# A four-layer graph network on one core: the layout of each stage hands out dense steps for longer past the planned end of the edge work (OVERHANG 3000 to 15000)

## The reference, cut to what matters

```
h = relu(layernorm(x)); x = x + gcn(h)      # weighted sum over edges, degrees of src
h = relu(layernorm(x)); x = x + sage(h)     # two SAGE convolutions, mean over dst
h = relu(layernorm(x)); x = x + mlp(h)      # message MLP per edge, mean over dst, update MLP, layernorm
h = relu(layernorm(x)); x = x + mean(h)     # mean over src, two matrices
```

## Time and profile before

| | us |
|---|---|
| median of three runs | 5219.02 |
| lowest, highest run | 5215.02, 5253.27 |
| the profiled execution, span from first to last instruction | 5223.6 |

### The profile page before, as it was taken

The page is one execution under the profiler, slowest core; times in us unless marked ns, Lnnn a source line. Parts: engine busy times, 40 slices in busy tenths (PEclk is TensorE's granted clock), DMA queues, the critical chain, the costliest instruction groups (busy, mean ns, idle before and its releaser), DMA issues. The chain is left out here.

```text
span 5223.6 us, 87376 instructions
## 1 busy us (share of the span) xinstructions
PE 3895.7 (75%) x22802; PEld 3063.3 (59%) x22802; DVE 4158.1 (80%) x20654; ACT 3626.8 (69%) x9152; POOL 3880.5 (74%) x3228
## 2 busy tenths in 40 slices
PE   5517877778676668999868978989788886666654
PEld 4415666666455556877756766766566665554443
DVE  7628999999999997777758878888799997766564
ACT  0027989888666766777758877878678886766564
POOL 6777787885677766888866777776588775777777
PEclk9868999999777788999989989999899998878777
DMA  9966777776666665666658889988466663333332
GB/s 229 321 192 191 197 211 203 195 201 159 161 152 154 147 139 143 164 152 158 143 136 260 237 224 245 247 236 210 126 147 144 144 139 74 102 98 98 96 96 62
DMA packets 891584, 878.75 MB, mean 168 GB/s; under 512 B 131160, under 2 KB 671714, under 8 KB 891016
## 3 DMA queue, kind: packets, MB, share of 16 engines
q1 hardware_dynamic: 546568, 575.48, 34.2%
q0 software_dynamic: 224000, 235.91, 26.1%
q10 hardware_dynamic: 120514, 61.79, 4.6%
HBM read 345.71 MB, written 533.16 MB: 168 GB/s over the span
## 5 line engine op out<-in xcount | busy, mean ns | idle before, releaser
L1206 POOL DMA_INDIRECT node<-sage_comb,leadd x400 | 644.7, 1612 | 203.5 <-DMA node<-sage_comb,leadd 104.0
L460 PE MATMUL dense_p<-ident,dense_h 128*128 128x128 f32 x1956 | 336.0, 300 | 373.4 <-ACT dense_h L454 367.1
L454 ACT ACTIVATE dense_h<-dense_x,dense_n_shift,dense_n_rstd 128x128 f32<-128x128 f32 x1304 | 534.8, 487 | 89.1 <-DVE dense_n_shift L443 85.7
L460 PEld LDWEIGHTS dense_p<-ident,dense_h 128*128 128x128 f32 x1956 | 239.8, 151 | 475.7 <-ACT dense_h L454 454.0
L1206 POOL DMA_INDIRECT sums<-mlp_same,leadh x200 | 325.2, 1626 | 139.0 <-issue 80.2
L1206 POOL DMA_INDIRECT node<-gcn_comb,leads x200 | 326.3, 1632 | 105.3 <-issue 49.2
L1206 POOL DMA_INDIRECT sums<-mean_comb,leads x200 | 328.0, 1640 | 95.8 <-DMA sums<-mean_comb,leads 45.7
L470 PEld LDWEIGHTS dense_p<-wT,dense_hT 128*128 128x128 f32 x2608 | 378.8, 209 | 22.8 <-issue 7.4
L470 PE MATMUL dense_p<-wT,dense_hT 128*128 128x128 f32 x2608 | 377.1, 292 | 0.0
L451 ACT ACTIVATE dense_n_std<-dense_n_mean_var,eps 128x4 f32<-128x4 f32 x652 | 188.8, 294 | 216.1 <-DVE dense_n_mean_var L437 213.9
L1041 ACT ACTIVATE dense_hT<-dense_p 128x512 f32<-128x512 f32 x489 | 286.2, 589 | 63.8 <-PE dense_p L460 60.8
(11 more groups left out here) (310 smaller groups left out, 14374.1 us busy)
## 6 DMA issues: line engine op xcount, KB each, us to landing
node<-b SPq DMA_DIRECT2D x400, 256.0 KB
sums<-zero_row SPq DMA_DIRECT2D x400, 256.0 KB
node<-zero_row ACTq DMA_DIRECT2D x50, 1152.0 KB
dense_x<-in_x SPq DMA_DIRECT2D x163, 256.0 KB, 3.3
out<-dense_y SPq DMA_DIRECT2D x163, 256.0 KB
x_src<-xs SPq DMA_DIRECT2D x50, 256.0 KB, 5.7
y_dst<-gcn_y SPq DMA_DIRECT2D x50, 256.0 KB, 3.1
sage_xs<-x_src SPq DMA_DIRECT2D x50, 256.0 KB, 3.9
```

Source lines behind the costliest of these rows:

```text
L454: tiles(lambda t: nc.scalar.activation(out[:, t, :], x[:, t, :], func, bias=b.sh[:, t:t + 1], scale=b.rs[:, t:t + 1])).then_inc(done, 1)
L460: return tiles(lambda t: nc.tensor.transpose(ps[:, t * P:(t + 1) * P], x[:, t, :], ident))
L1206: pool.indirect_dma_start(table, bass.IndirectOffsetOnAxis(ap=leads[:, i * G + c, t:t + 1], axis=0), e.comb[c][:, t, :], None, element_off ...
```

## The change

```diff
 PATIENCE = 100
-OVERHANG = 3000
+OVERHANG = 15000
```

## The result

The changed kernel took 5322.82 us (median of five runs, 5316.02 to 5352.36) against 5219.02 before: a ratio of 1.0179 with a 95% interval of 1.014 to 1.0218 (the ratios of this document are taken over the sets of runs; the quotient of the two medians is 1.0199). It is slower by 104 us, which lies outside the range and on the side of my third rival. The profiled execution has a span of 5350.6 us and was the slowest of the five, so differences between the two traces add up to 127 us, not 104. TensorE's clock isn't what differs: averaged over an execution the granted clock was 0.879 to 0.884 after, and 0.881 to 0.886 in the thirteen executions of the kernel before that ran beside experiments 1 to 4. (In experiment 3 it was 0.873 to 0.875, in experiment 6 0.885 to 0.887, and both are slower than before.)

What follows compares the result with a forecast made beforehand. POOL, nearly full in every stage, was taken as the bound, DVE as second limit. 5223.6 + 35 (ends) - 19 (mean) + 0 (re-laid plans) = 5239.6 us, less 4.6 above the median: 5235, range 5195 to 5285.

Steps and rivals of the forecast that it cites:

- third rival: A re-laid sage2 falls badly, its chain of adds not catching up: 61 us more, 5296 us; chance 0.22.
- The ends: Longer dense tails delay barriers: gcn +13, sage1 +13, sage2 0, mlp +9; together +35 us, bounds +31 and +41.
- cover: At sage2's end, POOL's last three groups of adds hide the 13 us of added dense work, so cost 0.
- DVE's stop: At sage2's end, DVE's idle 26.82 us should be cut to about 14.
- the term that I set to 0, the re-laid plans: sage1 to mean laid out anew from shifted dense streams; each stage taken to last as before, 0 us.
- Mean's slack of 37 us: Mean's edges last 687.8 us against 650.9 of POOL's busy time and minimum idle time.
- sage2's 18 us: Slack of sage2's edges: 660 us against 642 of POOL's busy time and minimum idle time.
- The bounds that I drew: Re-laid stages as tight as sage2: sage1 -61, mlp -66; as loose as sage1: sage2 +61, mean +43, mlp +20.
- the sign that this term decides: First gather to last add moving by over 20 us in sage1, sage2 or mlp: the re-laid-plans term decides.
- the sign that the gain is wrong: Mean's POOL gap, 21.25 us, should fall to about 9.4; staying over 15 means the gain is wrong.
- Mean's end: Four dense rounds fewer let dense work end some 94 us before the edges; next gather 12 us earlier.
- the edges would go faster in mean (-7): With mean's last 94 us free of dense steps, two groups of adds wait less for ACT: -7 us.

Runs made afterwards that it cites:

- experiment 1: Kernel before with its orders kept, only the dense steps of 12 more planned us moved ahead of the barrier at four ends: 5244.98 us against 5221.72, ratio 1.0036.
- Experiment 2: Changed kernel with its orders kept, but the added dense tails run after the barrier, at the next stage's front: 5311.26 us against 5221.72, ratio 1.0149.
- experiment 3: Kernel before, overhang 3000, each due time shifted by a fixed pseudo-random -100 to +100 ns: 5364.76 us against 5221.72, ratio 1.025.
- experiment 4: Kernel before with an overhang of 4000 in place of 3000: 5326.74 us against 5221.72, ratio 1.0165.
- experiment 6: Changed kernel (overhang 15000) with new due times for sage1 to mean, fitted by a search: 5279.7 us against 5227.39 for the kernel before, ratio 1.0091.
- experiment 10: Kernel before, overhang 3000, with other pseudo-random due-time shifts of -100 to +100 ns, on a slower chip: ratio 1.0233.
- experiment 9: Kernel before, overhang 3000 everywhere, with new fitted due times for mean alone, on a slower chip: ratio 1.0014, no difference.
- experiment 5: Kernel before with overhang 15000 at mlp's end only, so mean alone is laid out anew: 5300.56 us against 5227.39, ratio 1.013.
- experiment 8: Kernel before with overhang 15000 at sage2's end only and new fitted due times for mlp and mean: 5250.05 us against 5227.39, ratio 1.0034.

## Why the prediction was wrong

**The ends were right.** I had +13, +13, 0 and +9; the trace has +13.0, +9.0, +0.1 and +11.4, so 33.6 for my 35. The reading behind it held: a barrier that dense steps hold pays for each further one, and sage2's end had its cover. DVE's stop there fell from 26.82 us to 7.36 (I had 14; timeline of DVE):

```profile
2750.80 0.69 DVE L1004 TENSOR_TENSOR dense_y<-dense_p,dense_h 128x512 f32<-128x512 f32 x1 [1.52 <-PE dense_p L470]
2758.86 0.87 DVE L434 BATCH_NORM_STATS2 dense_n_stats<-dense_y 128x6 f32<-128x128 f32 x4 [7.36 <-PEq L897]
```

Experiment 1 puts this part at +23 us of the median.

Three small slips in the working change nothing. A dense round has 43 compute steps, not 37, so that with all hand-overs it is planned at 34 us and not 33.6. In the orders of experiment 1 the four tails hold 146 more dense steps, 3.2 rounds and not 4. And the lower bound of the ends adds up to +32, not +31.

**The step that failed is the term that I set to 0, the re-laid plans.** I wrote that the nearest row to a stage with another start is the stage itself. Experiment 2 gives the new orders their size, mean's late end included: +90 us of the median, with short tails. Experiments 3, 4 and 10 show why 0 was no neutral value: with one planned microsecond more of dense work, or due times off by 100 ns, the kernel is 1.7 to 2.5% slower. I also wrote that the trace can't show an order that hasn't run. The layout can: it is part of the kernel, and for the change it plans 122 us more. That sum was mine to take before the run. The layout picks, among steps that could begin within 100 ns of each other, the lowest due time. By the code, one swap moves all that follows, so that a small shift can give quite another order and not a nearby one. The order of before was an exceptional one among its neighbours: the four kernels that lay out several stages anew from its tables (the change, experiments 3, 4 and 10) are all planned over 110 us longer and measured over 100 us slower. Mean's slack of 37 us, which I had computed, may have been a sign of it: the same sum gives 55 to 79 in the change and in experiments 3 and 4. sage2's 18 us were none: its edges took 656 to 664 us under every order tried there, the slower chip of experiments 9 and 10 left out. The bounds that I drew (-127 to +124) hold what came, sage1 +22, mlp +14, mean +20; taking 0 between them was the error. Of my own signs, sage1's edges moved by over 20 us, the sign that this term decides, and mean's gap stayed over 15, the sign that the gain is wrong. The third rival named the mechanism and a chance of 0.22, but put it in sage2, the one re-laid stage whose edges hardly moved (-1.7 us), and had 61 us for it.

**Mean's end went the other way**, -12 predicted, +33 measured. I divided mean's length by its rounds and took four rounds off. Two steps of that are false. The dense work done in the tails wasn't kept: it was lost again in the re-laid stages, and 1275 dense steps were left for mean in place of 1253. And what ends last is a chain, not a sum: experiments 1 and 5 both have 1221 steps left, and gaps of 21.35 and 68.06 us. A dense stream at mean's end is as late as its own order against the edges lets it be. That the edges would go faster in mean (-7) fell with it (+20.1).

The order of before is better in the layout's own arithmetic already. Why its tables give so short a plan, and how they were found, stays open: numbers like these look like the outcome of a search, but nothing here shows it. Experiment 6, where fitting gives back half of the loss, shows that due times can be found for a long overhang too. It doesn't tell whether a longer search would give back all of it but the ends.

## What to carry to other kernels

Where a program lays out the order of its own instructions by a greedy rule and a table of priorities, every edit ahead of the layout is two edits: what it says, and a new draw of every order behind it. Read first what the layout itself plans for the new order, stage by stage: it costs no run, and here it had +122 us where the medians have +104, and the late end of mean. Then price the draw, by an edit that does nothing but nudge the table; here a nudge of 100 ns cost 2.3 to 2.5%, and the constant of the change, with the orders held fixed, cost 0.4%. Then refit the table before judging the constant, or hold the order fixed and move only the boundary.

## What the runs showed of the hardware

From the end of the last accumulating add to the next stage's first gather there are never less than 9.38 us in any trace (9.38 before, 9.50 after, 9.44 to 9.56 at the shortest end in each of experiments 1 to 5, 8 and 9): landing, semaphores and barrier together, five times in the program. No run splits them. The shortest gap was the same on a slower chip (9.49 and 9.52 in experiment 9).

That chip was the one of the last two experiments, where the kernel before took 6228.31 us for 5219.02 elsewhere, 19% more. The slowdown wasn't even: experiment 10 against 3, two nudges of the same kernel, had 1136.9 us for 794.4 in final, but 697.7 for 659.9 in sage2's edges. Its cause wasn't looked into, and whether ratios between two kernels carry over from one chip to the other isn't shown, since only the kernel before ran on both.
